# First keys loaded in the projection, mask terms spread, and two key tiles handled as one of 1024 columns

## The reference, cut to what matters

```python
x = x + ffn0(oscillator(cond, cond, drive=x))     # 256 RK4 steps in a row, then a gated FFN with a Hadamard
x = x + moe(attention(x, mask=cond_2048))         # 16 heads of 16 channels over 512 positions, then 8 experts, top 2

att = einsum('bhqd,bhkd->bhqk', Q, K) / sqrt(16) + b[0]
att = att * m + (1 - m) * -1e30                   # m = mask[b, k], any real number
att = softmax(att);  y = einsum('bhqk,bhkd->bhqd', att, V)
```

## Time and profile before

| | us |
|---|---|
| Median of 3 runs (2973.91 to 2975.04) | 2974.14 |
| The profiled execution's own time | 2969.96 |
| Its span | 2968.2 |

### The profile page before, as it was taken

The page is one execution under the profiler, slowest core; times in us unless marked ns, Lnnn a source line. Parts: engine busy times, 40 slices in busy tenths (PEclk is TensorE's granted clock), DMA queues, the critical chain, the costliest instruction groups (busy, mean ns, idle before and its releaser), DMA issues. The chain is left out here.

```text
span 2968.2 us, 111409 instructions
## 1 busy us (share of the span) xinstructions
PE 2532.7 (85%) x41104; PEld 1764.0 (59%) x41104; DVE 2464.3 (83%) x11808; ACT 1218.4 (41%) x4106; POOL 1557.6 (52%) x4198
## 2 busy tenths in 40 slices
PE   4478888888888888888888787999999988999999
PEld 4346666666666666666666654666666654444444
DVE  7989999999999999999999567999999976555454
ACT  3243333333333333333333247999999960000000
POOL 6845656566565666556655225777777765000000
PEclk7599999999999999999999998999999999999999
DMA  4100000000000000000000052111111110000000
GB/s 186 44 20 3 10 10 10 3 10 10 10 6 8 10 10 10 4 11 10 10 3 10 24 197 63 48 48 48 41 41 48 44 72 1 28 0 29 0 29 14
DMA packets 43608, 88.10 MB, mean 30 GB/s; under 512 B 7136, under 2 KB 23776, under 8 KB 41312
## 3 DMA queue, kind: packets, MB, share of 16 engines
q1 hardware_dynamic: 36048, 62.58, 6.5%
q10 hardware_dynamic: 4752, 10.49, 0.9%
q0 software_dynamic: 2304, 8.39, 0.9%
HBM read 64.66 MB, written 16.78 MB: 27 GB/s over the span
## 5 line engine op out<-in xcount | busy, mean ns | idle before, releaser
L228 PE MATMUL rest<-Tl,CW 128*128 128x56 f16 x16384 | 618.4, 190 | 316.3 <-DVE Tl L494 316.3
L228 PEld LDWEIGHTS rest<-Tl,CW 128*128 128x128 f16 x16384 | 503.1, 97 | 562.0 <-DVE Tl L494 558.3
L347 ACT ACTIVATE Tf<-X 128x32 f32<-128x32 f32 x768 | 176.1, 229 | 780.5 <-DVE X L538 780.5
L625 POOL TENSOR_TENSOR G<-X,Dr 128x32 f32<-128x32 f32 x768 | 205.9, 268 | 302.2 <-DVE X L499 274.4
L1138 DVE CUSTOM_DVE_ANT_0 negL<-Lps,negC 128x512 f32<-128x512 f32 x512 | 332.6, 684 | 35.5 <-PE Lps L1028 34.8
L1104 ACT ACTIVATE Pr<-negL,nM 128x512 f32<-128x512 f32 x512 | 340.8, 717 | 30.1 <-DVE nM L1138 29.8
L1041 PE MATMUL Tps<-idS,Pr 128*128 128x128 f32 x2048 | 290.9, 287 | 1.1 <-ACT Pr L1104 1.1
L217 PE MATMUL main<-Th,CW 128*128 128x56 f16 x8224 | 264.2, 189 | 10.3 <-DVE CW L450 10.3
L1041 PEld LDWEIGHTS Tps<-idS,Pr 128*128 128x128 f32 x2048 | 229.0, 145 | 60.9 <-issue 58.2
L1158 DVE TENSOR_TENSOR PT<-Tps,PT 128x512 f16<-128x512 f32 x384 | 252.7, 684 | 4.4 <-ACT PT L1112 3.9
L627 POOL TENSOR_SCALAR gm<-X 128x32 f32<-128x32 f32 x768 | 227.3, 296 | 43.0
(11 more groups left out here) (141 smaller groups left out, 5385.5 us busy)
## 6 DMA issues: line engine op xcount, KB each, us to landing
stage<-w_up SPq DMA_DIRECT2D x8, 1024.0 KB, 4.7
qk<-qkp ACTq DMA_DIRECT2D x32, 256.0 KB, 2.3
wstage<-moe_up POOLq DMA_DIRECT2D x16, 512.0 KB, 5.7
QR<-qk SPq DMA_DIRECT2D x128, 64.0 KB, 2.2
KR<-qk SPq DMA_DIRECT2D x128, 64.0 KB, 2.2
W2m<-w_down SPq DMA_DIRECT2D x1, 4096.0 KB, 13.3
stage<-x_tb SPq DMA_DIRECT2D x16, 256.0 KB, 2.7
x<-stage SPq DMA_DIRECT2D x16, 256.0 KB, 2.1
```

What stands on the lines that cost most here:

```text
L228: last = pe.matmul(rest[:, m], CW[:, 0, k, m * P:(m + 1) * P], Tl[:, k:k + 1, :].to_broadcast([P, REP, B]), start=(m == 0 and k == 0), sto ...
```

## The change

It has three edits, all in `attention`.

1. The first batch's Q and K are loaded by SyncE at the end of the projection block, once batch 0's four stores to `qk` have landed (`qk_out[0]` reaches 128: 64 given at the start and 64 by the stores), and not at the start of the attention block. For this `QR`, `KR` and their semaphores are made earlier, and `kf` lies in the memory of `wst`; so VectorE waits for its own last read of `wst` before it writes there.
2. The four operations of the mask term run in heads 3, 7, 11 and 12, one in each, and no longer one behind the other in head 12.
3. The banks `Tps[0]` and `Tps[1]` are one PSUM tensor of 2 x 512 columns, `Tpair`. ACT rounds both key tiles in one instruction, which waits for the transposes of both, and DVE subtracts both in one instruction, which waits for the end of ACT's. Tile 2 and tile 3 are as they were, and so is the order on every engine.

```diff
@@ attention, opening
-        negC = sb("negC", [P, 2, D])
+        negC = [sb("negC0", [P, D])]
+        QR = sb("QR", [P, NH // 2, D], F16)
+        KR = sb("KR", [P, NH // 2, D], F16)
+        qk_in = [sem("qk_in0"), sem("qk_in1")]
+        def load_qk(sp, b, half):                 # moved up, its body unchanged
+            for tensor, dst in ((0, QR), (1, KR)):
+                for par in range(2):
+                    for slot in range(4):
+                        part = slot % 2 if tensor == 0 else slot // 2
+                        row = par * 64 + slot * 16
+                        sp.dma_start(dst[row:row + 16, half * 4:(half + 1) * 4, :],
+                                     qk_heads[b, tensor, half, par, part]).then_inc(qk_in[half], 16)
@@ projection block
-            kf = sb1("kf", [P, 2, D])
+            kf = wst[:, 0:2].rearrange("p a c n -> p a (c n)")
@@ SyncE, behind its loop over the inputs
+                sp.wait_ge(qk_out[0], 128)
+                for half in range(2):
+                    load_qk(sp, 0, half)
@@ VectorE, ahead of the first mask terms
+                dve.wait_ge(w_lo, 1)
-                dve.scalar_tensor_tensor(negC[:, 0], ...
+                dve.scalar_tensor_tensor(negC[0][:], ...
@@ attention block
+        negC.append(sb("negC1", [P, D]))
-        Tps = [ctx.enter_context(nc.psum_tensor(f"Tps{i}", [P, 512], F32)) for i in range(4)]
+        Tpair = ctx.enter_context(nc.psum_tensor("Tps0", [P, 2, 512], F32))
+        Tps = [Tpair[:, 0], Tpair[:, 1]] + [ctx.enter_context(nc.psum_tensor(f"Tps{i}", [P, 512], F32)) for i in (2, 3)]
@@ SyncE of the attention block
             sp.dma_start(mrow[:], mask[1].partition_broadcast(P)).then_inc(in_mask, 16)
-            for half in range(2):
-                load_qk(sp, 0, half)
@@ GpSimd
-            def mask_terms(b):
-                ... all four operations, one behind the other
+            def mask_terms(b, part):
+                nc_b = negC[b % 2][:]
+                if part == 0:
+                    pool.wait_ge(in_mask, 16 * b)
+                    pool.wait_ge(s_neg, 64 * (b - 1) + AHEAD)
+                    pool.tensor_scalar(nc_b, mrow[:], -1.0, 1.0, ALU.mult, ALU.add).then_inc(negc_t, 1)
+                elif part == 1:
+                    pool.wait_ge(negc_t, 3 * b + 1)
+                    pool.tensor_scalar_mul(nc_b, nc_b, NEG).then_inc(negc_t, 1)
+                elif part == 2:
+                    pool.tensor_scalar(mt[:], mrow[:], b0S[:, 0:1], None, ALU.mult).then_inc(negc_t, 1)
+                else:
+                    pool.wait_ge(negc_t, 3 * b + 3)
+                    pool.tensor_tensor(nc_b, nc_b, mt[:], ALU.subtract).then_inc(negc_ok, 1)
-                if h == 12 and b + 1 < B:
-                    mask_terms(b + 1)
+                if h in (3, 7, 11, 12) and b + 1 < B:
+                    mask_terms(b + 1, (3, 7, 11, 12).index(h))
@@ ScalarE
+            def transposed_high_pair(b, h):
+                i = b * NH + h
+                act.wait_ge(s_T, i * DC + 2 + AHEAD)
+                act.wait_ge(s_pv, i - 1 + AHEAD)
+                act.activation(PT[:, h % 2, 0, 0:2, :], Tpair[:], ACT.Copy).then_inc(s_hi, 2)
-                for qt, kcs in ((0, ()), (1, (0, 1, 2)), (2, (3,)), (3, ())):
+                for qt, kcs in ((0, ()), (1, (2,)), (2, (3,)), (3, ())):
                     if real(j):
                         exps(*at(j), qt)
+                    if qt == 1 and real(j - 1):
+                        transposed_high_pair(*at(j - 1))
@@ VectorE
+            def transposed_low_pair(b, h):
+                dve.wait_ge(s_hi, (b * NH + h) * KD + 2 + AHEAD)
+                dve.tensor_tensor(PT[:, h % 2, 1, 0:2, :], Tpair[:], PT[:, h % 2, 0, 0:2, :], ALU.subtract).then_inc(s_lo, 2)
-                for kc in (0, 1):
-                    if real(j - 1):
-                        transposed_low(*at(j - 1), kc)
+                if real(j - 1):
+                    transposed_low_pair(*at(j - 1))
```

More of the change, by code:

```diff
@@ L840, in _ @@
                 dve.wait_ge(first_mask, 2)
-                dve.scalar_tensor_tensor(negC[:, 0], kf[:, 0], NEG, kf[:, 1], ALU.mult, ALU.subtract).then_inc(first_mask, 1)
+                dve.scalar_tensor_tensor(negC[0][:], kf[:, 0], NEG, kf[:, 1], ALU.mult, ALU.subtract).then_inc(first_mask, 1)
                 dve.wait_ge(first_mask, 3)
@@ L865, in attention @@
         idS = sb("idS", [P, P])
-        QR = sb("QR", [P, NH // 2, D], F16)
-        KR = sb("KR", [P, NH // 2, D], F16)
         mrow = sb("mrow", [P, D])
+        negC.append(sb("negC1", [P, D]))
         mt = sb("mt", [P, D])
@@ L878, in attention @@
         Lps = [ctx.enter_context(nc.psum_tensor(f"Lps{i}", [P, 512], F32)) for i in range(2)]
-        Tps = [ctx.enter_context(nc.psum_tensor(f"Tps{i}", [P, 512], F32)) for i in range(4)]
+        Tpair = ctx.enter_context(nc.psum_tensor("Tps0", [P, 2, 512], F32))
+        Tps = [Tpair[:, 0], Tpair[:, 1]] + [ctx.enter_context(nc.psum_tensor(f"Tps{i}", [P, 512], F32)) for i in (2, 3)]
         Ops = [ctx.enter_context(nc.psum_tensor(f"Ops{i}", [P, DC, 128], F32)) for i in range(2)]
-        in_id, qk_in = sem("in_id"), [sem("qk_in0"), sem("qk_in1")]
+        in_id = sem("in_id")
         in_mask, negc_t, negc_ok = sem("in_mask"), sem("negc_t"), sem("negc_ok")
@@ L894, in attention @@
         KD = DC - 1
[L896 to L904, removed]
         QKI = 16 * 16
@@ L1137, in negate_and_max @@
                 dve.wait_ge(s_exp, n - 3 + AHEAD)
-                dve.tensor_tensor_reduce(out=negL[:, qt, :], in0=Lps[qt % 2][:, :], in1=negC[:, b % 2], scale=1.0,
+                dve.tensor_tensor_reduce(out=negL[:, qt, :], in0=Lps[qt % 2][:, :], in1=negC[b % 2][:], scale=1.0,
                                          scalar=3.0e38, op0=ALU.add, op1=ALU.min,
```

## The result

| | us |
|---|---|
| Median after (3032.03 to 3038.54, 4 runs) | 3036.68 |
| Median before in the same comparison | 2974.27 |
| Ratio after to before | 1.0207, interval 1.0189 to 1.0225 |
| Profiled execution, its own time and span | 3035.16, 3033.4 |

The account below looks back on a forecast made before the run. DVE was taken to set the 4.72 us head, PE and ACT close behind. Double tile +65, mask terms -22 and first keys -12 gave +31: 3001 against the profiled execution, 3005 as median; 8-in-10 range 2982 to 3030 us.

Parts of the forecast that it names:

- The sign: Whole kernel: it becomes slower, by 31 us; slower was given a chance of 0.89.
- the round of waits: Attention, one head's score 3 on DVE to the next's: 4.49 us before against a head of 4.72, 5.23 after.
- the SBUF row of 1.41: DVE's 1024-column duration from SBUF, used only for the upper bound: head 5.47, +0.75 a head, 95 us.
- The new round: 1.93 + 1.12 + 1.05 + 1.13 = 5.23: Attention head with the double tile: score 3 to transposes, to ACT, to DVE, to score 3; +0.51 a head, +65 us.
- The sum: Whole kernel: double tile 65, mask terms -22, first keys -12, together +31 us.
- The longer gap lowers PE's clock in every head: Rival, attention: PE's gap of 0.74 lowers its clock, at least 1 us a head, over 3130 us; chance 0.05.
- Mask terms, -22 us: Attention, heads near 11 of each batch: spreading GpSimd's mask operations wins back the whole 22 us lost there.
- First keys, -12: Start of attention: the first score waits for `idS` only and starts 11.9 us earlier.
- the double tile pays as meant: Rival, attention: DVE keeps setting the head, at 4.65; -43 us in all, 2931 us; chance 0.07.
- Wide operations dear: Rival, attention: wide operations save nothing or cost more, head 5.47, +61 us in all, 3035 us; chance 0.08.

Follow-up runs that it names:

- e5: Kernel after with DVE's double subtraction moved behind score 3 instead of ahead of it; 2931.27 us, ratio to before 0.9866.
- e3: Kernel after, but ACT rounds tiles 0 and 1 one at a time; only DVE's subtraction stays double; 2966.05 us, ratio 0.9981.
- e6: Kernel after with ACT's double copy raising its semaphore by 1 instead of 2; 3016.47 us, in a second run 3013.86 us, ratio 1.0143.
- e9: Kernel after with both double operations, ACT's and DVE's, raising their semaphores by 1 instead of 2; 3004.47 us, ratio 1.0112.
- e8: Kernel after with six extra matmuls behind each head's values, their result unread, to fill PE's wait for DVE; 3023.77 us, ratio 1.0172.
- e1: Kernel after without the double tile: early keys and spread mask terms only, tiles 0 and 1 handled one by one; 2937.27 us, ratio 0.9886.
- e2: Kernel before with the double tile alone: late keys, the four mask operations together in head 12; 3050.85 us.
- e11: e1 with increments of 2 instead of 1 on ACT's three roundings and DVE's three subtractions, waits' counts doubled; 2937.69 us, ratio 0.9887.
- e10: e5 with both double operations raising their semaphores by 1 instead of 2; 2929.61 us, ratio 0.9864.

## Why the prediction was wrong in size

**The sign and the round of waits held.** That the round of waits, and not DVE's work, would set the head was right: DVE idle in front of the double subtraction (97.9 us in total, 70 forecast), released by ACT, and PE's wait for DVE grown. e5 shows it directly, e3 shows how it divides. ACT's double copy took 1.02, as taken; DVE's 1.22 and the turn 1.14, against 1.13. Taking the 1024-column durations from the slopes of narrower PSUM rows worked; the SBUF row of 1.41 would have misled.

**"The new round: 1.93 + 1.12 + 1.05 + 1.13 = 5.23" was short by 0.15, or 18 us.** This is the first of the two steps that failed. The prediction took ACT's start at 1.12 behind the transposes and DVE's at 0.03 behind ACT's end, from rows whose operations raise their semaphores by 1. Measured are 1.18 and 0.10. 0.12 of it is the increment by 2 that the change brings with it (e6, e9). The other 0.03 is left in e9 too, where ACT's start, DVE's start and the turn are each 0.01 longer than taken (1.13, 1.06, 1.14). The diff showed `then_inc(s_hi, 2)`, but no row of before had one, and I had set no bound for it.

**The sum had nothing for the clock.** This is the second step, and the other 13 of the missing 31 us. "The longer gap lowers PE's clock in every head" was put at 0.05 and priced as all or nothing; it happened in 19 of 124 heads and cost 13 us. (e8, where the clock stays up, is 50 us over its own before, the kernel after 62.) The one row of before had a gap of 1.87, and "0.74 is far from 1.87" is no argument about where between the two the clock gives way. The right reading was an unknown, with its own price in the range. And the two errors hang together: in e9, whose gap of 0.77 is near the forecast's 0.74, the clock stays at 1.00 in all steady heads.

**Mask terms, -22 us: right** where DVE sets the head (e1: 22.0 to 1.2). With the double tile edit 2 is worth about 4 (e2); the losses that it took away came back in part as heads with a lowered clock. **First keys, -12: right,** 12.3, at no cost to the projection.

Of the rivals, "the double tile pays as meant" fails in this order of work and holds with one move (e5). "Wide operations dear" fails: its 3035 is within 2 us of the measured 3036.68 by chance, for its head was 5.47 with DVE's operation at 1.41, where the trace has 5.38 and 1.23, and it had no lowered clock. The Trainium skill's rule that grouping can pay on a saturated engine (Perfetto Trace Analysis, Optimizing Scalar/DVE Operations) agrees with e5, where the wide operation has no one waiting: 0.06 us a head against e1. The other rule of that section, on breaking instructions up, is given there for engines that are not saturated but cause bubbles on others. In the kernel before DVE was saturated; only the merge made it idle, and there the rule fits what e3 shows, 0.43 us a head back for breaking up ACT's copy.

## What to carry to other kernels

- Before two operations are merged, follow the ring of waits that leads from the merged one round to itself, and compare it with the head's length: here there was 0.23 us of room, and the merge made the ring 0.89 longer. That an engine is saturated does not say that a merge on it will pay.
- A merged operation belongs where nothing short waits behind it: moving it past one other instruction turned +98 us into -6.
- When a wait grows on PE, put its clock into the range, also if the gap is much shorter than one that is known to lower it.

## What the runs showed of the hardware

- An operation that raises its semaphore by 2 and has been waiting starts later than with 1: by 0.05 us on ACT (1.18 to 1.13 behind the transposes in e6, 0.74 against 0.69 in e11 and e1), by 0.07 on DVE (0.10 to 0.03 behind ACT's end, medians of the steady heads of e6 and e9). On DVE without a wait it costs nothing (heads of 4.66 in e10 and 4.72 in e11, as in e5 and e1). Why isn't known; I had expected no difference.
- PE's clock went from 2.4 to 1.2 GHz (granted 0.50) 19 times in 124 heads at a gap of 0.89 us in 5.38. At 0.84 in 5.33 it did so once in two runs of 124 heads, behind a single gap of 1.21, and at 0.77 in 5.26 never. Whether it is the gap or PE's busy share that decides can't be told from these runs, as the two changed together.
